# Sixteen scatters and sixteen gathers of a routed expert layer, issued in one run each instead of in runs of eight

## What is computed

```python
logits = xt @ w_router                                   # xt: 2048 tokens x 128; 32 experts
probs = jax.nn.softmax(logits, axis=-1)
top1 = jnp.argmax(probs, axis=-1)
gate = jnp.take_along_axis(probs, top1[:, None], axis=1)[:, 0]
pos = jnp.cumsum(onehot, axis=0)[jnp.arange(T), top1] - 1
accepted = pos < C                                       # C = 80, so the first 80 tokens of an expert
slot = jnp.where(accepted, top1 * C + pos, E * C)
buf = jnp.zeros((E * C + 1, H), dtype=x.dtype).at[slot].set(xt)
...
y = jnp.einsum('ecf,efh->ech', jax.nn.silu(g) * u, w_down)
out_tok = y.reshape(E * C, H)[jnp.clip(slot, 0, E * C - 1)]
out_tok = jnp.where(accepted[:, None], out_tok * gate[:, None], 0.0)
return (xt + out_tok).reshape(B, S, H)
```

## Time and profile before

| | us |
|---|---|
| three runs: median (lowest to highest) | 1803.29 (1797.32 to 1804.77) |
| the profiled execution | 1801.73 |
| its span, from the first to the last record | 1799.8 |
| in the span: TensorE busy | 1530.6 (85%) |
| VectorE busy | 1013.2 (56%) |
| ScalarE busy | 868.9 (48%) |
| GpSimd busy | 632.9 (35%) |
| the switch experts' stage | about 835 to 936 |

### The profile page before, as it was taken

The page is one execution under the profiler, slowest core; times in us unless marked ns, Lnnn a source line. Parts: engine busy times, 40 slices in busy tenths (PEclk is TensorE's granted clock), DMA queues, the critical chain, the costliest instruction groups (busy, mean ns, idle before and its releaser), DMA issues. The chain is left out here.

```text
span 1799.8 us, 31587 instructions
## 1 busy us (share of the span) xinstructions
PE 1530.6 (85%) x11327; PEld 1135.4 (63%) x11327; DVE 1013.2 (56%) x2402; ACT 868.9 (48%) x1935; POOL 632.9 (35%) x707
## 2 busy tenths in 40 slices
PE   4689978799786999996939999899996799878996
PEld 3356655566573567774827877787875577635664
DVE  6656536666275789995035554466645123535555
ACT  5455544555356677772424444544443132235552
POOL 3487603877140667772230001100013501511113
PEclk8889988899997899998859999999997899969998
DMA  7300000000000834645224000000000201300000
GB/s 218 114 13 13 13 7 2 13 13 12 13 1 9 92 65 78 77 59 113 76 71 146 1 0 1 1 1 1 1 1 7 64 15 33 37 4 2 2 2 25
DMA packets 75277, 63.71 MB, mean 35 GB/s; under 512 B 25367, under 2 KB 62790, under 8 KB 75142
## 3 DMA queue, kind: packets, MB, share of 16 engines
q1 hardware_dynamic: 65142, 53.53, 14.7%
q0 software_dynamic: 3072, 6.30, 1.7%
q10 hardware_dynamic: 6928, 2.12, 0.6%
HBM read 48.09 MB, written 9.57 MB: 32 GB/s over the span
## 5 line engine op out<-in xcount | busy, mean ns | idle before, releaser
L1355 POOL TENSOR_TENSOR inject<-delta_x,b_rows 128x512 f32<-128x512 f32 x128 | 159.5, 1270 | 82.1 <-DMA b_rows<-b_rows_dram 44.7
L1626 DVE TENSOR_TENSOR_SCAN state<-bank,inject 128x512 f32<-128x512 f32 x128 | 150.3, 1205 | 7.0 <-POOL inject L1355 4.0
L2064 POOL TENSOR_TENSOR ve<-mv,eps 128x1 f32<-128x1 f32 x32 | 6.1, 190 | 338.6 <-DVE mv L2212 338.6
L1536 ACT ACTIVATE bank<-delta,a_neg 128x255 f32<-128x255 f32 x256 | 109.0, 472 | 13.4 <-DVE state L1626 12.9
L3324 DVE TENSOR_REDUCE top<-bank 128x2 f32<-128x512 f32 (+1 forms) x96 | 61.8, 685 | 72.7 <-PE bank L3026 51.8
L2173 ACT ACTIVATE Z<-bank 128x512 f32<-128x512 f32 x64 | 34.7, 595 | 127.7 <-PE bank L2126 127.7
L2150 ACT ACTIVATE U<-bank 128x512 f32<-128x512 f32 x128 | 74.7, 593 | 41.9 <-PE bank L2087 40.8
L595 POOL TENSOR_TENSOR rotated<-rot_cos,rot_sin 128x512 f32<-128x512 f32 x56 | 70.8, 1268 | 52.0 <-DVE rot_sin L901 52.0
L1441 PEld LDWEIGHTS bank<-tabs,by_token 128*128 128x128 f32 x512 | 67.9, 196 | 24.8 <-issue 15.7
L601 POOL TENSOR_TENSOR inv_norm<-sum_sq,neghalf 128x16 f32<-128x16 f32 x28 | 82.0, 2929 | 4.2 <-POOL sum_sq L599 0.2
L638 PE MATMUL bank<-wqkv,hT 128*128 128x512 f32 x128 | 68.7, 667 | 16.4 <-ACT hT L799 13.1
(11 more groups left out here) (565 smaller groups left out, 4214.8 us busy)
## 6 DMA issues: line engine op xcount, KB each, us to landing
b_rows<-b_rows_dram SPq DMA_DIRECT2D x32, 512.0 KB, 8.9
v<-v SPq DMA_DIRECT2D x32, 130.0 KB, 2.3
slots<-zero SPq DMA_DIRECT2D x10, 256.0 KB, 3.5
rows<-slots SPq DMA_DIRECT2D x10, 256.0 KB, 4.1
moe_w<-in_L_ffn_rg_dram SPq DMA_DIRECT2D x1, 2048.0 KB, 8.7
moe_w<-in_L_ffn_ru_dram SPq DMA_DIRECT2D x1, 2048.0 KB, 13.8
wqkv<-in_L_ffn_wqkv_dram SPq DMA_DIRECT2D x2, 768.0 KB
slots_out<-y SPq DMA_DIRECT2D x8, 160.0 KB, 2.1
```

The costliest lines, as they stand in the source:

```text
L1355: pool.tensor_tensor(dB[:, n % R, :, :], dx[:, :, seq(n)], both(b_all[:, q % 4, n % CH, :]), ALU.mult).then_inc(s.inject.sem, 1)
L1536: last = act.activation(dA[n % RD][:, c, 1:L], delta[:, c, i * L + 1:(i + 1) * L], ACT.Exp, scale=a_neg[:, c, k:k + 1])
L1626: dve.tensor_tensor_scan(flat(h[:, n % R, :, :]), flat(dA[n % RD]), flat(dB[:, n % R, :, :]), 0.0, ALU.mult, ALU.add).then_inc(s.state.sem, 1)
```

## The change

In the switch experts' stage GpSimd's wait between the eighth and the ninth scatter goes, and so do the four waits between the eighth and the ninth gather. SyncE's wait for all sixteen scatters and VectorE's waits for each batch stay. `RUN` remains in use in the two-choice stage, whose code is the same.

```diff
                 for t in range(NT):
-                    if t == RUN:
-                        pool.wait_ge(moved, 16 * t)
                     pool.indirect_dma_start(net.slots[0], bass.IndirectOffsetOnAxis(ap=scatter[:, t:t + 1], axis=0),
                                             net.x_tok[:, t * P:(t + 1) * P], None).then_inc(moved, 16)
                 pool.wait_ge(stored, 16 * STEPS)
                 pool.wait_ge(s.slots.sem, s.slots.at(0, 2))
                 for t in range(NT):
-                    if t == RUN:
-                        for batch in range(t // TPB):
-                            pool.wait_ge(arrived[batch], 16 * TPB)
                     pool.indirect_dma_start(yg[:, t, :], None, net.slots_out[0],
                                             bass.IndirectOffsetOnAxis(ap=gather[:, t:t + 1], axis=0)).then_inc(arrived[t // TPB], 16)
```

## The result

| | before | after |
|---|---|---|
| median of 20 runs of each, taken in turn | 1800.43 us (1795.46 to 1806.45) | 1804.97 us (1799.38 to 1809.01) |
| ratio after to before, 95% interval | | 1.0027 (1.0016 to 1.0038) |
| profiled execution, its span | 1801.73, 1799.8 us | 1804.57, 1802.8 us |

The change makes the kernel 0.27% slower, 4.5 us by the medians. The forecast was 2.9 us faster. The time lies within the range and within 0.5% of no change, but on the other side of before. The page's first line is

The account below looks back on a forecast made before the run. What ends last at two switch-stage joints was taken as the bound: TensorE's fold after the scatters, the gathers at the close. Scatters 0, gathers -2.9: -2.9 us, from a median of 1803.29 to 1800.4 us; range 1794.5 to 1806.

Parts of the forecast that it names:

- The waits' prices: GpSimd's queue in the switch stage: removing the pauses frees 2.15 us among the scatters and 2.93 us among the gathers.
- I cost this at nothing; the cover is the fold: Switch scatters: the 2.15 us saved count 0, since TensorE's fold ends at 877.6 either way and the rows have slack.
- (d): Rival at the scatters: earlier row loads collide with the fold and cost 1.44 us; -1.5 in all, 1801.8 us; chance 0.08.
- the low end: Switch gathers: gain of 2.0 us instead of 2.9 if the eighth gather's lateness is handed on to the ninth.
- (a): Rival at the gathers: transfers hand the wait on, late tiles being slow; gain 0 to -2, taken as -1, 1802.3 us; chance 0.12.
- (b): Rival: limited queue depth makes GpSimd wait inside each request from the ninth on; together +15, 1818.3 us; chance 0.04.
- (c): Rival at the scatters: the fold isn't the bound, so their 2.15 us count too; -5.1, 1798.2 us; chance 0.08.
- The 0.22 us that I set against it: Scatter joint: TensorE said to go from fold to transposes with 0.22 us between, evidence that the fold is the bound.
- a first transpose after 878.5: Sign of being wrong: TensorE's first transpose of the sorted rows, forecast at 877.6, starting later than 878.5.

Follow-up runs that it names:

- scatters_behind_folds: Kernel before without the wait among the switch scatters, the first scatter instead waiting until ScalarE has written out both folds; 1821.02 us (one run).
- before_again: The kernel before, unchanged, traced once more on the second chip; 1794.75 us (one run).
- gathers_only: Kernel before with only the waits among the switch gathers removed, first chip; 0.9984 (0.9969 to 1.0000), 1781.91 us against 1786.37.
- both_waits_gone: The whole change once more against the kernel before, on the second chip; 1.0019 (1.0007 to 1.0031).
- gathers_only_again: Kernel before with only the waits among the switch gathers removed, on the fourth chip; 0.9989 (0.9979 to 1.0000).
- scatters_only_again: Kernel before with only the wait among the switch scatters removed, on the fourth chip; 1.0044 (1.0031 to 1.0058).
- pause_by_memset: Kernel before with the switch scatters' wait replaced by a GpSimd clear of 128x2048, gathers keeping their waits, third chip; 1801.35 us (one run).

## Why the prediction was wrong, step by step

**The waits' prices: right.** 2.15 us leave GpSimd's scatters and 2.93 its gathers; measured are 2.2 and 3.1 in after, and where nothing else is late (first chip) the joints gain 2.0 and 2.9 us.

**"I cost this at nothing; the cover is the fold": the step that failed.** I asked what hides a gain of 2.15 us, and never what the wait protects. The fold ends behind the rows only because it is itself held up, and by the scatters. Counted from ScalarE's first copy it takes 23.3 us when left alone (scatters_behind_folds), 27.1 in before_again and 30.2 in before; and where nothing is late it is done 2.44 us before the rows (gathers_only). Without the pause in the middle the second eight of the scatters hold it up in one piece with the first: first transpose 6.1 us later in after, 9.5 in both_waits_gone, 8.7 with the scatters alone. The term of the sum was 0 and should have been about +6.

**The earlier trace rows were misread.** I saw two stalls of ScalarE with "remote" for a releaser and gave them to the loads of the weights, hence a bound of 1.44 us for (d). Beside the earlier trace rows they read otherwise. The first ended at 858.42, 1.4 us after GpSimd's eighth issue had; the second at 870.18, 0.9 us after the sixteenth had (868.32 plus 0.96). I subtracted the two as a large and a small case of one cause, the DMA load, and in scatters_behind_folds, with the same loads of weights, neither is there. Of the first alone a caution: la_q comes at 858.45 in after too, so this one stall didn't need the pause to end. What the pause ended is what follows it in after, 6.44 and 3.84 us more.

**The gathers: mechanism right, size off.** VectorE was free and the lag not handed on. But 2.9 was forecast, 2.0 taken as the low end, and 0.8 arrived in after. In the last three batches VectorE stands on "issue" and "remote", not on its rows, as the folds' engines do beside the scatters, and the low end didn't know of that. With the gathers alone it was worth 0.11% on the fourth chip, 2 us, its interval just reaching 1.

**The clock gave something back.** I looked at TensorE's clock at the gathers only. The end of before's second fold runs slowly: 32 matmuls in 5.13 us that take 2.82 us elsewhere, and in the fourteen us from 870 its granted clock is 0.63, against 0.86 in after. In after, behind its thin work from 857 to 870, TensorE has the faster clock, and the twenty transposes take 2.40 instead of 4.25 us, more than the 1.2 us that the stretch from first transpose to first gather is shorter. The +6.1 also has a gain of clock in it: 5.13 - 2.82 = 2.3 us in the last matmuls of the fold, so the stall by itself cost some 8.4 us, and in both_waits_gone, where before_again had the faster clock too, 9.5. The same 2.3 us are part of why the first transpose comes after 30.7 and 30.9 us in before and gathers_only_again and after 27.1 to 27.6 in three other kernels with the wait. What decides the clock from case to case these rows don't tell.

**Sum by these:** +6.1 (scatters) -1.2 (transposes) -0.8 (gathers) = +4.1 us, beside +4.5 in the medians.

**The rivals.** (a) is refuted: the queue hands no lateness on, and the lag was row 0. (b) is refuted: issues stay at 0.94 to 1.03 us and the landing at 2.5 to 2.6. (c) holds on the first chip, where the fold isn't held up. What (c) only guessed at, that the fold's stalls depend on the scatters' traffic, is what the runs found, but with a loss for the result where (c) had a gain. (The 0.22 us that I set against it are not in the earlier trace rows, where fold and transposes follow with no time between.) (d) named the right victim, but the row loads as culprit and 1.44 us as its limit; they go out at 868.40, when the stall is nearly over. My list of what would prove me wrong held "a first transpose after 878.5", and it did: it came at 883.73.

## What stays open

Which part of an indirect DMA delays the others, its issue by GpSimd or its transfer, is not settled. The runs show, on three chips of four: long stalls begin after some six issues 1.26 us apart, in the switch stage they end at the latest 0.9 to 3.1 us after the end of the last issue, a pause between two runs of eight lets the first fold through, and the pause needn't be a wait for landings. No instruction was loaded while the engines of after stood. In the two-choice stage of before the longest stall ended at 1428.44, in the middle of a run, so the end of a run is not the only thing that ends a stall. TensorE, ScalarE and VectorE are late alike, and SyncE's row loads are not. The Trainium skill names one link between these engines, in SBUF — State Buffer (Who interferes with whom): VectorE and GpSimd share a pair of ports under an exclusive lock, while TensorE and ScalarE have ports of their own and never wait. That rule doesn't account for these rows, where TensorE and ScalarE are the ones held up and VectorE does next to nothing (0.09 us in thirteen).

Why one chip of the four shows none of it is open too. Its 1786 us for the kernel before stand against 1800 to 1803 on the others; the two-choice stretch (68.7 to 53.7) and the first joint of the switch stage (30.7 to 26.3) give 19.4 us, more than the difference, so something else goes the other way. (Part of the 4.4 us at the switch stage's joint is TensorE's clock in before.) The whole change wasn't run on that chip, only its halves, which each gained 0.16%.

Gaps of 1.8 us between all scatters, and runs of six, weren't tried.

## What to carry to other kernels

When a wait is to be removed, ask what runs beside the issuing engine and whether its stalls end when the issuing pauses; work that shows "remote" or "issue" stalls on two or three engines at once is no cover, since it may be late only because of the queue that it is to hide. Break long runs of GpSimd's indirect DMAs by waits for their landings where other engines are on the path (runs of four gained 0.34% in the two-choice stage, and nothing in the switch stage), and let masked lanes of a gather read rows of their own (0.34% more). Measure a change of a few us on more than one chip: here the same edit of the scatters is -0.16% on one and +0.44% on another.

## What the runs showed of the hardware that I had not expected

Runs of eight and sixteen indirect DMAs hold up engines that share neither data nor semaphores with them: VectorE stands 13.6 us with its input ready (after), ScalarE up to 7.92 us at once (scatters_only_again), TensorE up to 3.36 us in a fold (pause_by_memset) and 7.26 us in the two-choice stage (after). Chips of one kind differ by 0.9% on one kernel (1786.4 and 1802.6 us), and the largest differences found lie where scatters run beside the other engines. A gather of which many lanes read one row of HBM keeps the DMA engines busy four times as long (49.6% to 12.5%) with about the same packets and bytes.
